# Holding GpSimd's passes for a gated tile until VectorE's routing is done

## The reference, cut to what matters

```python
# end of the mixer: y is the scan's output, u and z come from the input projection
mu, var = mean(y), mean(square(y - mu))
yn = (y - mu) * rsqrt(var + LN_EPS) * ln_g + ln_b
y = (yn + D_param * u) * silu(z)
x = x + y @ W_out.T
# expert network on the normalized tokens
xf = layernorm(x)
xa = xf @ P_w.T
C1, C2, C3 = (combine_weights(xa, U, k=3) for U in (U1, U2, U3))   # softmax over the top 3 of 12
h = gelu(sum_e C1[:, e] * (xf @ W1[e].T))
x = x + sum_e C2[:, e] * (h @ W2[e].T) + C3 @ b2
```

## Time and profile before

| what | value |
|---|---|
| median of three runs | 1942.43 us |
| the profiled execution | 1945.75 us, its span 1943.7 us |
| mean granted TensorE clock over the span | 0.928 of full speed |
| PE busy over the whole span | 1597.0 us (82%) |
| DVE busy | 1405.3 us (72%) |
| ACT busy | 1012.8 us (52%) |
| POOL busy | 542.6 us (28%) |
| stage that the change touches | from about 1572 us to the end of the span |

### The profile page before, as it was taken

The page is one execution under the profiler, slowest core; times in us unless marked ns, Lnnn a source line. Parts: engine busy times, 40 slices in busy tenths (PEclk is TensorE's granted clock), DMA queues, the critical chain, the costliest instruction groups (busy, mean ns, idle before and its releaser), DMA issues. The chain is left out here.

```text
span 1943.7 us, 37126 instructions
## 1 busy us (share of the span) xinstructions
PE 1597.0 (82%) x11024; PEld 1037.9 (53%) x11024; DVE 1405.3 (72%) x3794; ACT 1012.8 (52%) x2725; POOL 542.6 (28%) x556
## 2 busy tenths in 40 slices
PE   6999999999998997889894881776777746787899
PEld 3666666666664554555562771565556533333444
DVE  4777777777776666666675445999999976778776
ACT  2666666666664332232331227999999921221221
POOL 1111111111111010000000111988888856223100
PEclk9999999999999998999896995889888866889999
DMA  4101110111005500000563001000000000000000
GB/s 131 34 22 32 32 32 22 32 32 32 22 22 173 174 0 1 1 0 0 150 202 109 0 0 61 1 1 1 1 1 0 0 0 1 1 6 6 11 6 17
DMA packets 69345, 66.53 MB, mean 34 GB/s; under 512 B 5695, under 2 KB 66834, under 8 KB 69266
## 3 DMA queue, kind: packets, MB, share of 16 engines
q1 hardware_dynamic: 66598, 64.00, 11.1%
q10 hardware_dynamic: 2668, 1.62, 0.3%
HBM read 61.41 MB, written 4.19 MB: 34 GB/s over the span
## 5 line engine op out<-in xcount | busy, mean ns | idle before, releaser
L1968 PE MATMUL ss_y_ps<-ss_h,ss_diag 128*128 128x256 f32 x1024 | 265.3, 423 | 132.9 <-ACT sc_dt L1886 92.7
L1968 PEld LDWEIGHTS ss_y_ps<-ss_h,ss_diag 128*128 128x128 f32 x1024 | 216.5, 215 | 181.4 <-issue 94.6
L595 ACT ACTIVATE x_probs<-x_probs,x_neg_max 128x257 f32<-128x257 f32 x512 | 253.5, 498 | 64.0 <-DVE x_neg_max L696 64.0
L696 DVE CUSTOM_DVE_ANT_0 x_probs<-x_s_ps,x_mask_b 128x257 f32<-128x257 f32 x512 | 187.3, 423 | 134.9 <-PE x_s_ps L403 134.9
L1870 ACT ACTIVATE ss_decay<-sc_dt,sc_a 128x256 f32 (+1 forms) x496 | 206.7, 470 | 1.8 <-DVE ss_h L1933 1.8
L1924 DVE SCALAR_TENSOR_TENSOR ss_decay<-ss_decay,ss_h 128x1024 f32<-128x1024 f32 x124 | 152.3, 1229 | 28.5 <-ACT ss_decay L1870 28.2
L1880 ACT ACTIVATE ss_come<-ss_dtu,sc_xd 128x256 f32<-128x256 f32 x384 | 162.9, 505 | 6.6 <-POOL ss_dtu L1826 6.6
L413 PE MATMUL x_pT_ps<-all_ident,x_probs 128*128 128x128 f32 x1024 | 163.3, 283 | 0.6 <-DVE x_pT L703 0.6
L1840 POOL TENSOR_TENSOR ss_diag<-all_ident,sc_xd 128x512 f32<-128x512 f32 x128 | 159.8, 1249 | 11.4 <-PE ss_y_ps L1968 1.4
L703 DVE COPY x_pT<-x_pT_ps 128x512 f32<-128x512 f32 x256 | 161.3, 668 | 0.5 <-PE x_pT_ps L413 0.5
L1933 DVE CUSTOM_DVE_ANT_0 ss_h<-ss_come,ss_decay 128x1024 f32<-128x1024 f32 x124 | 150.0, 1210 | 0.0
(11 more groups left out here) (371 smaller groups left out, 3134.8 us busy)
## 6 DMA issues: line engine op xcount, KB each, us to landing
x_ctx_t<-ctxT SPq DMA_DIRECT2D x48, 514.0 KB, 3.8
kept_ctx_t<-ctxT SPq DMA_DIRECT2D x16, 514.0 KB, 7.9
kept_ctx_n<-ctx SPq DMA_DIRECT2D x16, 512.0 KB, 8.2
x_ctx_n<-ctx SPq DMA_DIRECT2D x16, 512.0 KB, 4.2
all_x<-x SPq DMA_DIRECT2D x4, 512.0 KB, 7.5
x_mid<-all_x SPq DMA_DIRECT2D x32, 64.0 KB, 4.0
all_x<-x_mid SPq DMA_DIRECT2D x4, 512.0 KB, 7.8
out<-all_x SPq DMA_DIRECT2D x8, 256.0 KB, 2.0
```

Source lines behind the costliest of these rows:

```text
L595: ins = nc.scalar.activation(probs[p][:, n, :], probs[p][:, n, :], ACT.Exp, scale=-1.0, bias=neg_max[p][:, n:n + 1], accum_out=sums[p][:, ...
L696: vec.tensor_tensor_reduce(probs[p][:, n, :], s_ps[:, c, 0:S2], mask_b[:, :], -1.0, -MASKED, ALU.add, ALU.min, neg_max[p][:, n:n + 1]).the ...
L1968: ins = nc.tensor.matmul(y_ps[p][:, 0:DI], diag[q][:, m, :], h[q][:, m, :], start=(q == 0 and m == 0), stop=(q == NQ - 1 and m == NH - 1))
```

## The change

One wait is added to GpSimd's program. From m = 3 on, the fourth group, it stands ahead of `skips(m)`, and so ahead of `finish(m)` too: GpSimd goes on when `route` has reached (m-2)·ROUTE_STEPS, that is when VectorE has done the routing of groups 0 to m-3. For m = 3 that is group 0's routing, which VectorE does ahead of the main loop; for m from 4 on it is the routing that VectorE does during the experts of group m-4. No instruction that computes is added, removed or altered, and the program of no other engine is touched.

```diff
@@ -2129,6 +2129,8 @@
             skips(1)
             finish(1)
             for m in range(2, NG):
+                if m > 2:
+                    pool.wait_ge(route, (m - 2) * ROUTE_STEPS)
                 skips(m)
                 finish(m)
 
```

## The result

The changed kernel takes 1896.64 us (median of four runs, 1896.01 to 1898.72) where the kernel before took 1942.67 beside it (1942.41 to 1943.51): a ratio of 0.9764, 95% interval 0.9747 to 0.9781. The profiled execution took 1898.72 us, its span 1896.6, at a mean granted clock of 0.939 (before 0.928). The change adds two lines at L2132, so every line behind them has a number two higher: the norm is L2396, the scale L2460, `turn_x` L2166, the expert L2195.

A forecast was written before the change was run, and what follows sets the result against it. VectorE's split, standing under GpSimd's passes, was taken to bound the second halves of groups 0 to 3. Halves 39.4 plus start 2.7 gave 42.1 us, taken from the median 1942.43: 1900.3 us, range 1897 to 1912.

The forecast's parts named there:

- The halves: Second halves of groups 0 to 3 become as group 4's, 14.91 us each, saving together 39.4 us.
- Where the passes go and what they meet: Main loop, m = 4 to 7: norms fall among short passes, end some 1.0 us late within 1.7 free, costing nothing.
- the start's last term: Stage's start, m = 3: group 1's norms done 3.6 us earlier, less 0.9 for the clock, gaining 2.7 us.
- The clock's term: In the start: 0.9 us subtracted for one more pair of expert matmuls at the lower clock (1.71 - 0.86).
- Rival B: Groups 1 to 4: each of four norms stands for a whole pass; 7.1 us slower, 1949.5 us; chance 0.03.
- The range's low end: Whole kernel: 1897 us, below which nothing is left to gain but group 0's shorter half.
- A: Four starts: last norms miss the short passes and wait for `ln_g`, 2.3 us late each; 1911.9 us; chance 0.16.
- C: At the added wait: routing is over before `finish` is released, so nothing changes; 1942.4 us; chance 0.02.

The follow-up runs named there:

- the loop-only kernel: The change with only the four main-loop waits (m = 4 to 7), none at m = 3: 1903.98 us, ratio 0.9808 to the kernel before.
- the kernel with the passes behind the norms: The change with m = 4 to 7 waiting on the next group's norms instead of the routing: 1897.64 us, ratio 0.978 to the kernel before.
- skip passes free: The change with its wait moved between skips and finish, so the skip passes are not held: 1915.31 us, ratio 0.9862 to the kernel before.
- the first comparison: The changed kernel's first measurement beside the kernel before: 1896.64 us against 1942.67, ratio 0.9764.
- in the second: The unaltered change measured once more in a later set, against the kernel before: 1898.69 us, ratio 0.9779.
- the passes at the norms: The change plus a second wait for m = 4 to 7, on the 24th scale of group m-4: 1910.42 us, ratio 0.9841 to the kernel before.

## Why the prediction was off by 3.7 us

*The halves were right.* Forecast 11.28, 10.87, 10.67 and 6.60 us, measured 11.15, 10.74, 10.66 and 6.59: 39.4 against 39.1. They became what group 4's was, the clock included, and the loop-only kernel shows the same 39.2 by itself.

*Where the passes go and what they meet was right.* The offsets behind the release were read as +2.42, +4.77 and +7.19 for the second skip pass and the short ones; they are +2.43, +4.78 and +7.05. Ahead of the norms stand six scales (I had counted five) and, from group 1 on, a sum. The norms are done 6.33 us behind the split's end (1664.55 - 1658.22), 0.4 later than in group 4; I had allowed 1.0. L2363 (L2361 before) stood for a skip pass in the start, as forecast, and had its cover:

```profile
1624.72 2.17 DVE L2363 SCALAR_TENSOR_TENSOR tl_sh<-tl_lnw,tl_rs 128x8 f32<-128x8 f32 x1
1627.44 0.69 DVE L2460 TENSOR_TENSOR tl_scaled<-tl_xnT,tl_w_ps 128x512 f32<-128x512 f32 x1 [0.55 <-remote]
```

*The step that failed is the start's last term:* "I take 3.6, nearer to the row of such norms, less 0.9 for one more pair of expert matmuls at the lower clock (1.71 - 0.86): 2.7." Its first half holds: `turn_x` of group 1 starts 60.77 us behind the stage's first instruction instead of 64.60, a gain of 3.83. The clock's term has the wrong sign: behind `turn_x` another 1.70 us were gained, together 5.53 instead of 2.7. The term asked how many matmuls would run at the lower level, and not why TensorE was at that level. The clock around the idle 4.26 us in the kernel before, in two stretches with the columns of the earlier trace rows, and then in the change from its rise to the end of the start:

```profile
1632.10:1635.45 3.35, 0.93 (x3) 0.09 (x1) 3.35 (x5) 0.23 (x1) 3.13 (x3) 1.00 0.00 0
1635.55:1642.25 6.70, 4.96 (x13) 3.23 (x14) 5.17 (x9) 1.20 (x2) 6.27 (x3) 0.50 0.01 2
```

```profile
1632.75:1649.55 16.80, 16.64 (x63) 8.48 (x62) 10.09 (x48) 3.46 (x6) 5.95 (x3) 1.00 0.00 1
```

Before, the grant was already 1.00 when TensorE ran out of work at 1633.03. It fell during the idle time, at 62.8 us into the stage, and came back at 69.6, 5.0 us behind `turn_x`. In the change the lower level ends 1.7 us behind `turn_x` and doesn't return in the start. That is 3.4 us less at half the speed, worth 1.7 us of work, and 1.70 were measured. So the lower level that I counted on was mostly the stall's own, and went with it. Rival B's sum has such a fall ("2.9 for the clock that falls in the stall"); the start's term doesn't give it back. The pair of expert matmuls ahead of `turn_x` did run at the lower level, but `turn_x` starts only 0.1 us later than in the kernel with the passes behind the norms, where it waits for the norms and not for that pair.

The kernel with the wait at m = 3 alone shows 5.4 by itself; the two in which the norms of group 1 still meet long passes (loop only, skip passes free) show 84.8 and 84.7, as before. In all twelve profiled executions the two go together: where TensorE idles for 3.5 to 4.3 us ahead of this `turn_x` (four of them), the lower level lasts for 4.9 to 5.2 us behind it (in three of them the grant fell in the idle time, with the skip passes free it had not risen before); where it idles for 0.4 or less (eight), for 1.7 at most. What sets the moment of a fall or a rise is not shown.

*The range's low end was argued wrongly.* It allowed the start "3.6 plus about 1 of clock", 0.9 less than came. "Below 1897 there is nothing left to gain" summed only what the stage can gain. With the start at its right size the sum is 44.7 us, 1897.7 from a median of 1942.4; the measured medians differ by 46.0 in the first comparison and by 43.2 in the second, while the stage gains 44.7 and 44.6 (both against the one profiled execution of the kernel before). So of the 3.7 us some 2.6 are the stage's, and about 1 us either way comes from outside it, where executions differ by up to 5 us; the range should have left room for that. The change took 1896.64 us in the first comparison and 1898.69 in the second, single runs 1896.01 to 1900.55; on which side of 1897 it came out was luck.

*The rivals.* A is a real mechanism with the price that I gave it for each start (2.3 us; 2.1 to 2.7 measured), but its condition was not met: VectorE is at its norms when the short passes run. B has half of its mechanism: norms do stand for whole passes where long ones meet them, two at a time and not four in the loop. C's condition was not met in the change. With the wait put one routing earlier it was met for `finish`, and even then the held skip passes gave 10.8 us: there the rival's "nothing would change" doesn't hold.

## What to carry to other kernels

When two engines disturb each other, list the short instructions of one that stand under the long ones of the other, and price each by its shortest and longest time in one line of the profile; a wait of a few characters then decides where the long ones go. Put them where the disturbed engine runs what does not stand, and order them so that the short passes fall on what can't be moved. The stretch in which the disturber is absent (group 4 here) gives the size of the gain in advance, the clock with it. Where there is no such stretch, as in the start, read the granted clock ahead of, in and behind the stall: a lower level that began in the stall goes with it.

## What the runs showed of the hardware

A stall of TensorE can cost more than its length. In the kernel before the grant fell from 1.00 to 0.50 (1.2 GHz) in the 4.26 us without work and stayed there for 5.0 us behind `turn_x`; without the stall it was 0.50 for 1.7 us, and the difference was worth 1.7 us. When the grant rises in the start varies: 59.3 to 62.5 us into the stage in executions of kernels whose start is the same.

How many VectorE instructions get through at a GpSimd pass's end is not always one, and here it goes by the pass that ends. In the change two norms took 1.25 us together behind the second skip pass; those at 1658.37 with the passes at the norms, behind the first, took 4.14. Over the twelve profiled executions a second norm got through behind the second skip pass (L2106) all 31 times and behind `ln_g` (L2117) all 10 times; behind the first skip pass (L2103) and the skip sum (L2120) it stood for the next pass all 4 and all 10 times. Behind L2106 a short pass follows; behind L2117 the next pass starts 0.14 us later, behind L2103 and L2120 0.08. That these gaps are the reason is not shown.

Very small instructions stand as long as large ones: a step of 128x4 elements took 2.18 us under a skip pass and 0.16 without.
